# Graph network kernel: low parts of dense chunks on ScalarE, dense chunks earlier in the order, pieces loaded up to two turns ahead

## The reference, cut to what matters

```python
h = relu(layernorm(x))                       # x: 6250 nodes x 128
msg = h[dst] @ W_i + h[src] @ W_j + edge_attr @ W_e      # 106250 edges, sorted by dst
agg = segment_sum(edge_weight[:, None] * msg, dst)
x = x + agg + h @ W_self
h = relu(layernorm(x))
for W_l, b_l, W_r in (layer1, layer2):       # relu after the first
    mean = segment_sum(h[src], dst) / max(count(dst), 1)
    h = mean @ W_l.T + b_l + h @ W_r.T
out = x + log_softmax(h)
```

## Time and profile before

| | |
|---|---|
| three runs | 1626.91, 1631.67, 1635.6 us |
| the profiled execution | 1629.45 us, span 1627.6 us |
| TensorE (PE) | 1400.3 us busy, 86% of the span |
| VectorE (DVE) | 980.0 us, 60% |
| GpSimd (POOL) | 726.9 us, 45% |
| ScalarE (ACT) | 600.8 us, 37% |
| the last sum of the first stage is added | at 972.08 us |
| the first large product starts | at 1015.38 us |
| mean granted TensorE clock | 0.95 of full speed |

### The profile page before, as it was taken

One profiled execution on the slowest core, in us unless ns is written; L12 is line 12 of the kernel. 1 busy time (PEld: TensorE's weight loads), 2 busy tenths in 40 slices (PEclk: granted clock), 3 DMA queues, 4 the chain that ended last, 5 costly groups with the idle time before them and its releaser, 6 DMA issues.

```text
span 1627.6 us, 25952 instructions
## 1 busy us (share of the span) xinstructions
PE 1400.3 (86%) x8448; PEld 1001.9 (62%) x8449; DVE 980.0 (60%) x4423; ACT 600.8 (37%) x1479; POOL 726.9 (45%) x783
## 2 busy tenths in 40 slices
PE   2587787798888887988879996999999979999996
PEld 0366566666666665656656666666666646666664
DVE  7799999998898997979889769100101030010204
ACT  5355665555656555455564336100000010020203
POOL 8777777777676776667666748000000000000000
PEclk9699999899999998989989999999999989999999
DMA  7478777899989898899889983778686838777773
GB/s 259 157 224 275 245 264 256 278 300 303 329 266 310 283 286 289 274 304 285 293 283 328 309 287 156 277 268 331 231 328 233 327 140 318 268 297 276 288 286 132
DMA packets 178853, 441.26 MB, mean 271 GB/s; under 512 B 24619, under 2 KB 104924, under 8 KB 175388
## 3 DMA queue, kind: packets, MB, share of 16 engines
q1 hardware_dynamic: 155996, 391.75, 67.0%
q0 software_dynamic: 22432, 46.97, 11.0%
q10 hardware_dynamic: 288, 0.85, 0.2%
HBM read 318.94 MB, written 120.55 MB: 270 GB/s over the span
## 4 chain that ended last, share of the span: by engine, by line
PE 62%; DVE 15%; DMA 9%; ACT 8%; POOL 2%; issue 2%; SPq 1%; DVEq 0%; ACTq 0%; POOLq 0%
PE psAE L1120 33%; PE psAE L1030 13%; DMA home<-h_table 8%; PE psAE L1062 6%; DVE home L1420 5%; ACT home L789 5%; DVE home L1424 4%; PE psW L931 3%; DVE home L1478 3%; PE psW L1049 2%; PE psW L1039 2%; ACT home L821 1%; PE psNS L1039 1%; ACT home L832 1%; POOL home L630 1%
## 5 line engine op out<-in xcount | busy, mean ns | idle before, releaser
L630 POOL DMA_INDIRECT home<-h_table,src_i x676 | 654.0, 967 | 257.8 <-issue 200.5
L1120 PE MATMUL psAE<-home 128*128 128x350 f16 x3528 | 539.3, 313 | 5.7 <-DVE home L1522 3.7
L1120 PEld LDWEIGHTS psAE<-home 128*128 128x128 f16 x3528 | 338.0, 96 | 201.8 <-issue 3.7
L1030 PE MATMUL psAE<-home 128*128 128x256 f32 x1352 | 324.3, 399 | 33.4 <-DVE home L1454 19.8
L1030 PEld LDWEIGHTS psAE<-home 128*128 128x128 f32 x1352 | 269.2, 201 | 86.0 <-issue 41.1
L1478 DVE TENSOR_SCALAR home<-iota_h,dst_rel,home 128x128 f32<-128x128 f16 x832 | 221.6, 363 | 17.9 <-PE psAE L1030 15.6
L1420 DVE TENSOR_SCALAR home<-iota_h,tile 128x245 f16<-128x245 f16 x1004 | 209.6, 302 | 27.5 <-PE psW L1049 18.6
L789 ACT ACTIVATE home<-psW 128x490 f16<-128x490 f32 x406 | 206.1, 578 | 49.8 <-PE psW L1039 40.3
L1424 DVE TENSOR_SCALAR home<-iota_h,tile 128x128 f16<-128x128 f16 x1004 | 179.4, 281 | 0.0
L1582 DVE SCALAR_TENSOR_TENSOR home<-psAE,home 128x350 f32<-128x350 f32 x18 | 9.4, 523 | 242.9 <-PE psAE L1120 238.1
L1582 DVE SCALAR_TENSOR_TENSOR home<-psAE,unscale,home 128x350 f32<-128x350 f32 x18 | 10.5, 582 | 239.5 <-PE psAE L1120 239.5
(11 more groups left out here) (211 smaller groups left out, 1220.3 us busy)
## 6 DMA issues: line engine op xcount, KB each, us to landing
home<-counts SPq DMA_DIRECT2D x36, 4287.5 KB, 13.5
counts<-home SPq DMA_DIRECT2D x126, 612.5 KB
home<-edges SPq DMA_DIRECT2D x64, 845.0 KB
weighted<-home SPq DMA_DIRECT2D x24, 1225.0 KB, 7.1
home<-weighted SPq DMA_DIRECT2D x36, 800.0 KB
home<-h_table,src_i POOLq DMA_INDIRECT x676
home<-h_table SPq DMA_DIRECT2D x36, 256.0 KB
home<-inv_row SPq DMA_DIRECT2D x36, 175.0 KB, 13.1
```

The lines of the kernel that those rows point to most:

```text
L630: pool.indirect_dma_start(out=rows[to][:, j, :], out_offset=None, in_=from_table[:, :], in_offset=bass.IndirectOffsetOnAxis(ap=src_i[b][:, ...
L1030: done = nc.tensor.matmul(psA[:, 0:2 * P].rearrange("p (n f) -> p n f", n=2), onehot[:, j, :], both_of(s, b, j), start=(j == 0), stop=(j = ...
L1120: last = nc.tensor.matmul((psA, psE)[r][:, 0:SNODES].rearrange("p (c d) -> p c d", c=SUPER), halves[:, a, n, :], tiles[:, :, a, :], start= ...
```

## The change

Three things. (1) For W2, W3 and W4 ScalarE makes the low parts too, so its `weigh_hots` has eight instructions in place of four there; VectorE makes low parts for W0 and W1 alone. (2) The dense chunks come at nearly even distances, the last one (D11) behind g38, in turn 50, and the spans of the pieces move with them: group 2 now has turns 52 to 62. (3) A piece's load is issued up to two turns ahead of its use, where its buffer is free by then; it was always issued one turn ahead. By the lists that the code computes, 32 of 39 loads now go out two turns ahead, among them those of all eight dense turns with a piece.

```diff
-DENSE_AFTER = (2, 5, 9, 12, 16, 19, 23, 27, 30, 34, 38, 41)
-PIECE_SPANS = ((14, 29), (29, 43), (43, 51))
+DENSE_AFTER = (2, 5, 8, 11, 15, 18, 21, 25, 28, 32, 35, 38)
+PIECE_SPANS = ((13, 27), (27, 40), (40, 51))
...
+TURN_OF = {piece: i for i in PIECES_AT for piece in PIECES_AT[i]}
+LOADED_AT = {i: [] for i in range(CHUNKS)}
+for _g, _n in sorted(TURN_OF):
+    _i, _free = TURN_OF[_g, _n], TURN_OF[_g, _n - 2] if _n >= 2 else WHEN[DSUPER * _g + DSUPER - 1] + 1
+    LOADED_AT[max(_i - 2, min(_i - 1, _free))].append((_g, _n))
...
-                    for g, n in PIECES_AT[i + 1]:
+                    for g, n in LOADED_AT[i]:
                         load_piece(g, n)
...
                 for j in range(4):
                     t, at = divmod(c * GROUPS + 4 * k + j, P)
-                    done = nc.scalar.activation(whot_all[k % 2][:, j, 0, :], ghot(4 * k + j)[1], ACT.Copy, scale=w_parts[t][:, 0, at:at + 1])
+                    for n in range(1 if k < 2 else 2):
+                        done = nc.scalar.activation(whot_all[k % 2][:, j, n, :], ghot(4 * k + j)[1], ACT.Copy, scale=w_parts[t][:, n, at:at + 1])
                 done.then_inc(whot_ready, 1)
...
                 pe.wait_ge(whot_ready, ORDER[i] * 5 + k + 1)
-                pe.wait_ge(whot_low, ORDER[i] * 5 + k + 1)
+                if k < 2:
+                    pe.wait_ge(whot_low, ORDER[i] * 2 + k + 1)
...
                     if half == 0:
                         node_weights(i, c)
-                        if i and ORDER[i - 1] < DENSE:
-                            low_hots(i - 1, (4,))
...
                 for k in ks:
-                    if c * 5 + k >= 2:
-                        dve.wait_ge(made, slot_end(i, "W", k - 2) if k >= 2 else slot_end(WHEN[c - 1], "W", k + 3))
+                    if c:
+                        dve.wait_ge(made, slot_end(WHEN[c - 1], "W", 4 - k))
...
                 add_sums(i, c, base)
-                if c < DENSE:
-                    low_hots(i, (2, 3))
```

## The result

The changed kernel took 1646.72 us, the median of six runs (1639.17 to 1654.73), against 1632.43 us (1626.91 to 1636.66) in six runs of the kernel before on the same chip. The ratio is 1.007, with a 95% interval of 1.0045 to 1.0095: slower by 0.7%, where 1627 was predicted. Its profiled execution took 1654.73 us, the longest of the six. The same kernel, run again in a later comparison as `changed_again`, gave 1.004 (1.002 to 1.006). Its profiled execution took 1643.60 us, the shortest of its twelve (median 1650.86), so the two traces of this kernel bracket it: its usual execution lies between them.

The account below looks back on a forecast made before the run. VectorE's pace was taken to bound the first stage, GpSimd's gathers the stretch behind the last dense chunk. Walk changes won nothing there, the stage's end -4 us: 1629.45 - 4 = 1625.4, median 2.2 higher, 1627.6; predicted 1627, range 1613 to 1640.

Parts of the forecast that it names:

- The chain through W4: Dense chunks: ScalarE's four added instructions for W4 lie on the chain, 1.26 us in each of 12, +15.1 us.
- The first rival: Dense chunks: VectorE's relief counts and ScalarE's added work is hidden, so the 15.1 us go, 1612.5 us; chance 0.17.
- The early loads: Dense turns and those behind: late pieces' cost goes, -27.7 us, less +4.8 us for the pieces' own time.
- about 20.5 at most with a piece: Turns behind dense ones: about 20.5 us at most with a piece, 19.7 us without one.
- The new order and the end of the stage: First stage: D11 ahead of g39 leaves nine chunks to gather, nothing won; the whole change gives -4 us.
- Up to the add behind D11: Turns up to D11: three gathered turns fewer plus the other terms put that add at 807.9 us, from 851.15.
- The sum ahead of GpSimd's last wait: Behind D11's add: a sum starts 0.4 us later and takes 5.8 us, so GpSimd's wait ends at 814.1.
- Nine chunks behind the last wait: GpSimd behind D11: 117 gathers without a wait take 147.7 us, the last ending at 961.8.
- The end of the stage: Behind the last gather: rows land in 1.8 us, scaling starts at 962, scaled add follows at once; -5.9 us, against up to +2.15.
- fourth rival: Change does less than it says: seven of 39 loads stay one turn ahead, reload may stay late; 1630 us, chance 0.10.
- The clock rival: Dense chunks: TensorE's clock drops in the longer wait before W4, eight matmuls take 1.7 us; +8.4 us, 1636 us, chance 0.15.
- slower rival: Dense turns: DMA engines are full, so pieces land as late as before; 22.9 us come back, 1650.5 us; chance 0.16.

Follow-up runs that it names:

- load_act23: `load_only` with ScalarE also making the low parts of W2 and W3, not of W4; ratio 0.9830 to the kernel before.
- load_only: The kernel before with piece loads up to two turns ahead alone, old order, low parts on VectorE; ratio 0.9809 to the kernel before.
- before_order_load_act: The changed kernel with the old order of dense chunks and old piece spans (D11 behind g41); ratio 0.9921 to the kernel before.
- d11_back: The changed kernel with only D11 put back behind g41, D0 to D10 as in the change; ratio 1.0011 to the kernel before.
- after_without_act: The changed kernel with the low parts back on VectorE, new order and early loads kept; ratio 0.9936 to the kernel before.
- order_only: The kernel before with the new order of dense chunks and new piece spans alone; ratio 1.0079 to the kernel before.
- reload_late: The changed kernel with SyncE's reload of the own rows held until half the last sum is done; ratio 1.0037 to the kernel before.
- load_first: `load_only` with the piece ahead of all slots of a dense turn, right behind the edge sums; ratio 0.9883 to the kernel before.

## Why the prediction was wrong

**The chain through W4: right.** W4 waits 2.49 us (forecast 2.5), the turns behind dense ones without a long piece take 19.6 to 19.8 us in `changed_again` (forecast 19.7), and VectorE waits 7.89 us (over 5). The forecast of 15.1 us measured 12.7 alone and 18 with the early loads. The first rival is false: `load_act23` took work from VectorE and won nothing.

**The early loads: right in direction, the size open.** Net -22.9 us was forecast. By the ratios it was -31 alone and -26 on top of ScalarE's part; the profiled executions of `load_only` and of the kernel before are 22.8 us apart. Of the 27.7 us that the prediction put down to late pieces, 25.0 lay in the dense turns and those behind them. The other 2.7 lay in the gathered turns, which take 11.95 us on average there and not 11.82, and which no load shortens. The sub-step "about 20.5 at most with a piece" failed: the six turns behind a dense one with a long piece take 22.3, 23.4, 20.7, 22.0, 21.2 and 20.5 us in `changed_again`, 130.2 in place of 6 x 20.5 = 123.0. In five of the dense turns ahead of them (D4, D5, D6, D8, D10) ScalarE waited 4.7 to 5.9 us for the counts, which the text named only as a late transfer that would show.

**The new order and the end of the stage: these steps failed.** The whole was forecast at -4 us, and the other two parts at -27.7 + 15.1 + 4.8 = -7.8. So the order with the end of the stage was to cost 3.8 us: 11.3 for the last gather, which comes at 961.8 and not at 958.3 - 7.8 = 950.5, less 7.5 that the end of the stage was to give back. It cost 20 to 24 us, and 13 alone. Point by point (us):

| | forecast | `changed_again` | late by |
|---|---|---|---|
| the add behind D11 | 807.9 | 815.5 | 7.6 |
| GpSimd's last wait ends | 814.1 | 824.9 | 10.8 |
| the last gather ends | 961.8 | 972.8 | 11.0 |
| the last sum starts | 963.6 | 977.9 | 14.3 |
| the last add | 970.4 | 986.8 | 16.4 |
| the first scaled add | 970.8 | 992.0 | 21.2 |

- *Up to the add behind D11:* the 7.2 us that the six turns above took too long are nearly all of the 7.6. They are no price of the order in this pair: the same six turns take as long in `before_order_load_act` (130.1).
- *The sum ahead of GpSimd's last wait* was taken at 5.8 us, from the turn behind D3. It took 8.53. The trace of the kernel before had this: its add behind D11 and the end of its last wait are 859.95 - 851.15 = 8.8 us apart, not 6.2, and its sum there took 8.00 us (granted clock 0.73 from 851.5 to 860):

```profile
851.67 8.00 PE L1030 MATMUL psAE<-home 128*128 128x256 f32 x26 [2.35 <-DVE home L1454]
```

- *Nine chunks behind the last wait* were forecast at 147.7 us and took 147.9. So the bound that I set behind D11 held, for this kernel.
- *The end of the stage gave nothing back.* The rows of the last gather were to land in 1.8 us, as in the first turn, where the DMA share was 0.15; they took 5.1 and 5.5. The last sum was charged up to +2.15 us for its wait; it took 2.05 and 2.87 more. The 7 us of a piece in the way thus went into landing and clock. And the scaling did not start early: GpSimd waited for the node weights, which TensorE transposes behind the last sum, and started at 987.9 instead of 962, so the scaled add came 5.2 us behind the last add and not at once. In the earlier trace rows that wait is put down to the own rows, the last of its releasers only. My fourth rival had a stage end without its gain, but on another ground, the late reload.

Set against `before_order_load_act`, the order costs 14.8 us at the last gather (forecast 11.3) and 2.3 us more behind it, where 7.5 were to come back. Of the 13.3 us that the forecast of the order missed in this pair, 9.8 lie in the end of the stage.

**What the order does ahead of D11, which the forecast put at nothing.** GpSimd needs 16.44 us a chunk. A period of one dense chunk and three gathered ones gives it about 13.9 + 19.7 + 2 x 11.8 = 57.2 us for 49.3 us of gathers, so it waits 8; with four gathered ones it has 69.0 for 65.8 and waits 3. In `changed_again` it waits 9.3, 11.6, 7.7, 9.6, 6.0 and 9.0 us right behind D3, D5, D6, D8, D10 and D11, each of which has three gathered chunks ahead of it, and 5.3, 3.7 and 4.9 us behind D4, D7 and D9, which have four. The new order has eight such short periods, the old one five. For the changed kernel the forecast had these waits counted, in the nine chunks left behind D11; for `d11_back` they explain how it can be slow with D11 back in its place. That the waits and the end of the last gather move together (31.9 and 32.1 us from `load_only` to `after_without_act`, 14.0 and 14.8 from `before_order_load_act` to `changed_again`) follows from the fixed total of gathers and names no cause by itself.

The add behind D11 should come 35.5 us earlier by the order. Between `before_order_load_act` and the two traces of the changed kernel it comes 36.1 and 28.2 us earlier, between the kernel before and `order_only` 25.1, and between `load_only` and `after_without_act` 17.4. So in three of four pairs the turns themselves grew longer, by 7 to 18 us. The cause stays open: ScalarE's waits for the counts grew by 13.5, 1.2 and 13.5 us in these three, but by 18.8 in the pair whose turns did not grow, and single executions scatter by several us.

**The clock rival: right in kind, small in size.** In the kernel before W4 took 1.00 us in all twelve turns. In `changed_again` it took 1.06 to 1.80 us in four of them, 1.7 us more in all, and in the first trace 1.14 to 1.80 in six, 3.4 us more; 8.4 were priced. In the Trainium skill, "TensorE: Matmul & The Clock Gate", Part 1 says that throttled is the default and activity releases it. The trace agrees with the direction: the mean granted clock is 0.937 over twelve executions, against 0.941 of the kernel before in the same comparison. The larger prices were paid in two pieces (4.20 and 4.55 us instead of 2.95) and in the last sums, behind waits of 9.08 and 7.73 us.

None of the rivals was the mechanism that decided, and none had the order as its cause. The slower rival had a sign and a size like the result (1650.5), but its cause, late pieces, is refuted by `load_only`.

## What to carry to other kernels

When one engine has a fixed total of work and finishes last, count its waits over the whole stage: every wait early on moves the end, even where the turn it lies in looks faster. Take each duration on that path from the place where it will be paid: here a sum of 8.0 us was taken at 5.8, and a landing of over 5 us at 1.8. Don't book a gain behind the last wait before every releaser of the next step is known. Test the parts of a change one at a time: here one part won 1.9% and the other two gave it all back.

## What the runs showed of the hardware

The sum that needs the rows of an indirect gather started 1.8 us behind it with the DMA share at 0.15 (the first turn) and 5.1 to 5.5 us behind it in the changed kernel, with the share at 0.97 to 1.00 meanwhile; with the reload held back (`reload_late`) it was 3.5 us, at a share of 0.52. A write of two counts blocks (612 KB each) held its buffer for up to 7.6 us past the point where ScalarE wanted it (6.88 in the changed kernel, 7.61 in `load_first`). TensorE's 26-product sum took 5.77 us at full clock, and 7.82 and 8.64 behind waits of 7.73 and 9.08 us.
